# A row of lane numbers in PSUM for one-hots, and GCN rows gathered once per tile

## The reference

```python
# layer 0: relations; rel = edge type, 8 of them
row = src + n * rel
deg = segment_sum(ones, row, r * n);  msg = x[dst] * (1.0 / deg)[row][:, None]
agg = segment_sum(msg, row, r * n).reshape(r, n, e)
out0 = relu(einsum('rij,rnj->ni', weights, agg))

# layer 1: GCN
deg = 1.0 + segment_sum(ones, dst, N);  dinv = rsqrt(deg);  h = x @ W
msgs = (dinv[src] * dinv[dst])[:, None] * h[src]
agg = segment_sum(msgs, dst, N) + h / deg[:, None]
out1 = batch_norm(leaky_relu(agg + b))
```

## Time and profile before

| what | value |
|---|---|
| median of 3 runs | 4256.2 us (4242.35 to 4259.15) |
| the profiled execution, its own time | 4245.88 us |
| its span, first to last instruction | 4244.1 us |
| granted TensorE clock, mean | 0.821 of full speed |
| busy: TensorE, VectorE, GpSimd, ScalarE | 74%, 63%, 59%, 19% |
| instructions | 59998 |

### The profile page before, as it was taken

One profiled execution on the slowest core, in us unless ns is written; L12 is line 12 of the kernel. 1 busy time (PEld: TensorE's weight loads), 2 busy tenths in 40 slices (PEclk: granted clock), 3 DMA queues, 4 the chain that ended last, 5 costly groups with the idle time before them and its releaser, 6 DMA issues. The chain is left out here.

```text
span 4244.1 us, 59998 instructions
## 1 busy us (share of the span) xinstructions
PE 3122.9 (74%) x14813; PEld 1957.0 (46%) x14814; DVE 2654.0 (63%) x8500; ACT 801.6 (19%) x2009; POOL 2499.5 (59%) x2771
## 2 busy tenths in 40 slices
PE   6988976636666635999997899965676876667773
PEld 3445865424444421444443344453354663345652
DVE  8986754351111249788887888884375774365875
ACT  3840000010000003000000677650010110010111
POOL 0027777737777605766663788703777751777760
PEclk8985556768888857999998999987887987889886
DMA  1111222221111112666662222203687863677871
GB/s 63 51 49 45 56 56 56 54 47 51 51 51 51 42 31 64 173 166 166 164 169 72 62 69 67 60 7 106 182 237 193 257 199 87 182 215 216 254 227 48
DMA packets 383723, 466.66 MB, mean 110 GB/s; under 512 B 56179, under 2 KB 284944, under 8 KB 383482
## 3 DMA queue, kind: packets, MB, share of 16 engines
q0 software_dynamic: 84864, 219.09, 20.9%
q1 hardware_dynamic: 298618, 244.58, 19.0%
HBM read 349.37 MB, written 114.10 MB: 109 GB/s over the span
## 5 line engine op out<-in xcount | busy, mean ns | idle before, releaser
L1844 POOL DMA_INDIRECT got<-kv_table,pair_src x832 | 824.7, 991 | 552.9 <-issue 368.1
L603 POOL DMA_INDIRECT y_got<-y_table,y_idx x416 | 450.0, 1082 | 404.7 <-POOLq L57 278.2
L1009 POOL DMA_INDIRECT got<-t_table,pair_src x416 | 412.6, 992 | 192.8 <-issue 126.2
L2055 PE MATMUL psum<-acc 125*128 x1664 | 288.0, 327 | 204.5 <-DVE h L1907 180.2
L1203 PE MATMUL sums<-msg,hot 128*125 128x512 f32 x832 | 404.5, 635 | 29.4 <-POOL msg L1144 29.4
L2067 PE MATMUL psum<-h,acc 128*128 128x128 f32 x1664 | 331.2, 335 | 77.2 <-ACT hot_b L2031 53.1
L1431 POOL DMA_INDIRECT got<-x_table,pair_src x312 | 294.3, 943 | 154.9 <-issue 152.0
L2055 PEld LDWEIGHTS psum<-acc 125*128 125x128 f32 x1664 | 248.2, 227 | 280.6 <-issue 279.5
L1019 DVE TENSOR_TENSOR hot<-pair_dst,iota 128x500 f32<-128x500 f32 x112 | 76.0, 684 | 457.2 <-PE gcn_psum L1085 456.8
L1470 DVE SCALAR_TENSOR_TENSOR small<-z,att 128x128 f32<-128x128 f32 x1248 | 287.0, 286 | 94.0 <-PE z L1535 94.0
L1907 DVE TENSOR_TENSOR h<-psum,got 128x512 f32<-128x512 f32 x208 | 143.1, 688 | 316.6 <-DMA got<-kv_table,pair_src 284.7
(11 more groups left out here) (490 smaller groups left out, 5724.5 us busy)
## 6 DMA issues: line engine op xcount, KB each, us to landing
v_rows<-got SPq DMA_DIRECT2D x208, 256.0 KB, 3.8
small<-v_rows SPq DMA_DIRECT2D x208, 256.0 KB
dst_row<-dst_rows SPq DMA_DIRECT2D x312, 125.0 KB
rows<-x_rows SPq DMA_DIRECT2D x104, 256.0 KB, 2.6
x_rows<-got SPq DMA_DIRECT2D x104, 192.0 KB, 2.1
got<-kv_table,pair_src POOLq DMA_INDIRECT x832, 4.1
y_table<-y_stage SPq DMA_DIRECT2D x25, 500.0 KB
y_got<-y_table,y_idx POOLq DMA_INDIRECT x416, 2.6
```

Of the source, the lines that this page charges most:

```text
L603: pool.indirect_dma_start(out=got[:, slot, j, :], out_offset=None, in_=y_table[:, :], in_offset=bass.IndirectOffsetOnAxis(ap=m.y_idx[:, co ...
L1009: pool.indirect_dma_start(out=self.got[:, slot, j, :], out_offset=None, in_=self.table[:, :], in_offset=bass.IndirectOffsetOnAxis(ap=self. ...
L1844: pool.indirect_dma_start(out=got[:, slot, j, :], out_offset=None, in_=kv_table[:, :], in_offset=bass.IndirectOffsetOnAxis(ap=m.pair_src[: ...
L2055: last = t.matmul(work[:, j * P:(j + 1) * P], hot_t[:, g % 2, j // 2, j % 2, :], m.acc[:, bass.ds(ws[j], 1), 0:D].rearrange("q o d -> q (o ...
```

## The change

1. Counting compares against a copy of the row of lane numbers in a PSUM bank (`ps[2]`), the GCN one-hots against one in a bank of their own (`iota_psum`).
2. GCN rows are gathered once per tile: 392 gathers by `tile_src` (made in `sort_edges`, one more operation there) in place of 416. They go into a ring of NS = 12 groups of four tiles, and a pair's product reads the slot (p - window) mod 48, a number that VectorE works out before (`slot_i`) and TensorE loads into a register, as it does the window's. Gather group g waits until pair group g - 6 is used. TensorE waits for tile group g before pair group g, and for nothing from group 98 on.
3. The 6 matmuls of zeros stay only behind pair groups 0 to 91.
4. The GCN loops of TensorE and VectorE are written out in place of loops of 13 rounds.
5. The ring of layer 0 has 33 groups, not 34, which also starts its `keep_busy` two groups earlier.

```diff
-YS, Y_EARLY, SL, RB = 6, 6, 34, 104
+YS, Y_EARLY, SL, RB = 6, 6, 33, 104
+NS, ROOM = 12, (W - 1) // 4
...
             dve.wait_ge(lanes_done, 1)
+            go(v.tensor_scalar(m.tile_src[:, :], lanes[0][:, 0:TILES], float(N - 1), None, ALU.min))
...
+            link(v.tensor_copy(ps[2][:, 0:P], m.iota[:, 0:P]))
             for g in range(groups):
...
-                v.tensor_tensor(hot_c[:, g % 4, :, :], bc_last(src_loc[:, g * G:(g + 1) * G], P), bc_mid(m.iota[:, 0:P], G),
+                v.tensor_tensor(hot_c[:, g % 4, :, :], bc_last(src_loc[:, g * G:(g + 1) * G], P), bc_mid(ps[2][:, 0:P], G),
...
-            loop.gathers(pool, lambda g, slot: pool.wait_ge(used, g + 1))
+            for g in range(tile_groups):
+                if g >= NS:
+                    pool.wait_ge(used, g - NS + ROOM + 1)
+                for j in range(G):
+                    col = g * G + j
+                    pool.indirect_dma_start(out=got[:, col % ring, :], out_offset=None, in_=table[:, :],
+                                            in_offset=bass.IndirectOffsetOnAxis(ap=m.tile_src[:, col:col + 1], axis=0)
+                                            ).then_inc(come[g % NS], 16)
...
+            def one_hots(g):
+                v.tensor_tensor(hot[:, g % 8, :, :], bc_last(m.pair_dst[:, g * G:(g + 1) * G], Q), bc_mid(iota[:, 0:Q], G),
+                                ALU.is_equal).then_inc(hot_ready, 1)
+
+            link(v.tensor_copy(iota[:, 0:Q], m.iota[:, 0:Q]))
+            link(v.tensor_tensor(slot_f[:, :], m.iota[0:1, 0:PAIRS], m.pair_win[0:1, :], ALU.subtract))
+            link(v.tensor_scalar(turn_f[:, :], slot_f[:, :], 1.0 / ring, 0.5 / ring - 0.5, ALU.mult, ALU.add))
+            link(v.tensor_scalar(turn_f[:, :], turn_f[:, :], ROUND, None, ALU.add))
+            link(v.tensor_scalar(turn_f[:, :], turn_f[:, :], ROUND, None, ALU.subtract))
+            link(v.scalar_tensor_tensor(slot_f[:, :], turn_f[:, :], -float(ring), slot_f[:, :], ALU.mult, ALU.add))
+            v.tensor_copy(slot_i[:, :], slot_f[:, :]).then_inc(slots_ready, 1)
+            for g in range(8):
+                one_hots(g)
...
+            pe.wait_ge(slots_ready, 1)
+            for g in range(groups):
+                ws = windows(nc, m.pair_win_i, ENG.PE, g * G, G)
+                at = windows(nc, slot_i, ENG.PE, g * G, G, ring - 1)
+                pe.wait_ge(hot_ready, g + 1)
+                if g < tile_groups:
+                    pe.wait_ge(come[g % NS], 16 * G * (g // NS + 1))
+                for j in range(G):
+                    last = t.matmul(sums[0:Q, bass.ds(ws[j] * D, D)], hot[:, g % 8, j, :],
+                                    got[:, bass.ds(at[j], 1), :].rearrange("l o d -> l (o d)"), start=False, stop=False)
+                last.then_inc(used, 1)
+                if g < tile_groups - ROOM:
                     keep_busy(t, sums[0:Q, 6 * 512:7 * 512], zeros, Q, 6)
             clear_banks(t, zeros, sums, True).then_inc(done, 1)
```

More of the change, by code:

```diff
@@ L212, in common @@
     m.pair_win = sb("pair_win", [P, PAIRS])
+    m.tile_src = sb("tile_src", [P, TILES], U32)
     m.pair_win_i = sb("pair_win_i", [1, PAIRS], I32)
@@ L978, with windows @@
 WG = 2 * G
-def windows(nc, wins, engine, at, n):
+def windows(nc, wins, engine, at, n, top=W - 1):
     cols = slice(at, at + n) if isinstance(at, int) else bass.ds(at, n)
     _, values = nc.values_load_multi_w_load_instructions(
-        wins[0:1, cols], engines=[engine], min_val=0, max_val=W - 1, skip_runtime_bounds_check_because="a pair's window is a count of 24 comparisons")
+        wins[0:1, cols], engines=[engine], min_val=0, max_val=top, skip_runtime_bounds_check_because="a pair's window is a count of 24 comparisons")
     return values
@@ L1033, in gcn_sums @@
         sb, sem, bank = scope(nc, ctx)
-        loop = PairLoop(nc, m, ctx, table, hots=8)
+        ring, come, groups, tile_groups = NS * G, m.come_tile, PAIRS // G, TILES // G
+        got, hot = sb("got", [P, NS * G, D]), sb("hot", [P, 8, G, Q])
+        slot_i, slot_f, turn_f = sb("slot_i", [1, PAIRS], I32), sb("slot_f", [1, PAIRS]), sb("turn_f", [1, PAIRS])
+        hot_ready, slots_ready = sem("hot_ready"), sem("slots_ready")
         zeros = sb("zeros", [P, 512], BF16)
-        sums = m.gcn_psum
+        sums, iota = m.gcn_psum, bank("iota_psum")
         used, zeroed, done = sem("used"), sem("zeroed"), sem("all_summed")
@@ L1053, in _ @@
         def _(pool):
-            loop.gathers(pool, lambda g, slot: pool.wait_ge(used, g + 1))
+            for g in range(tile_groups):
[6 more added lines that the diff above has]
+                                            ).then_inc(come[g % NS], 16)
+            for i in range(NS):
+                pool.wait_ge(come[i], 16 * G * ((tile_groups - i + NS - 1) // NS))
         @block.vector
@@ L1058, in _ @@
             nc.vector.memset(zeros[:, :], 0.0).then_inc(zeroed, 1)
-            for slot in range(loop.slots):
-                loop.one_hots(slot * G, slot)
+            v = nc.vector
             link = make_link(dve, chain)
+            def one_hots(g):
[10 more added lines that the diff above has]
+                one_hots(g)
             dve.wait_ge(loaded, 48)
@@ L1065, in _ @@
             link(nc.vector.tensor_tensor(m.x_beta[:, :, :], m.x[:, :, :], bc_mid(m.gcn_vec[0:Q, 2, :], W), ALU.add))
[L1066 to L1070, removed]
+            for g in range(8, groups):
+                dve.wait_ge(used, g - 7)
+                one_hots(g)
             dve.wait_ge(done, 1)
@@ L2157, in build @@
         common(m, sb)
-        m.come = [[sem(f"come{n}_{b}") for b in range(8)] for n in range(4)]
+        m.come = [[sem(f"come{n}_{b}") for b in range(8)] for n in range(3)]
+        m.come_tile = [sem(f"come_tile{b}") for b in range(NS)]
         m.come_y = [sem(f"come_y{b}") for b in range(SL)]
```

## The result

The changed kernel takes 4196.2 us (median, 4194.04 to 4197.35) against 4249.3 us of the kernel before measured beside it: a ratio of 0.9874, 95% interval 0.9847 to 0.9901, 53 us less. The forecast was a ratio of 0.9886 and 4208 us in a range of 4192 to 4234. The profiled execution has a span of 4194.1 us, 50.0 us less than before, where the sum said 48.5.

A forecast was written before the change was run, and what follows sets the result against it. GpSimd's gathers, lengthened by VectorE operations with both inputs in SBUF, were taken to bound layer 0's queue and the GCN sum. Terms -20.2 and -28.3 us gave -48.5, ratio 0.9886, 4208 us; range 4192 to 4234.

The forecast's parts named there:

- The bound and the mechanism: Layer 0's queue and the GCN sum follow GpSimd; one-hots with both inputs in SBUF lengthen gathers from 0.94 to 1.40 us.
- Layer 0: Sorting and layer 0 together: -22.0 us of counting's lead, +1.2 lost again, +0.6 for sorting, so -20.2 us.
- The catch-up: Layer 0's main loop: TensorE starts waiting for rows 8 groups later, at group 57, about 600 us; costs 1.2 us.
- the extra operation: Sorting: one more VectorE operation from PSUM, 392 columns, adds 0.6 us.
- GCN gathers: GCN sum: 24 fewer gathers, -29.9 us, and less lengthening by one-hots, net -11.1 us.
- the operations for slot_i: GCN start: new VectorE operations of some 3 us, covered, that may hold up gathers by 1.0 us.
- The GCN end: Last GCN gather to TensorE's end: landing, seven groups at half clock and clearing, 19.5 us, so +12.7 us.
- The landing: GCN end: rows of the last gather reach TensorE 1.8 us after it.
- the stages behind are unchanged: Everything after the GCN sum keeps its time: 0 us.
- A: Counting and GCN: a PSUM operand doesn't free the gathers; total -15.6 us, 4241 us; chance 7%.
- C: GCN sum: TensorE becomes the bound through loads and register operations; 4304 us at 5.8 us per group; chance 4%.
- B: Layer 0: counting's lead is lost again by a full ring, TensorE at half clock or slow landings; 4228 us; 7%.

The follow-up runs named there:

- gcn_psum: Kernel before with only the GCN one-hots reading the row of lane numbers from PSUM: 4238.6 us, ratio 0.9963.
- count_psum_2: Kernel before with only counting's one-hots reading the row of lane numbers from PSUM, on a chip of normal speed: 4228.5 us, ratio 0.9943.
- wide_psum: Changed kernel with the three wide GCN operations (3200 columns) reading their small operand from PSUM copies: 4197.2 us, 3.7 us under the changed kernel's repeat.
- both_more: Changed kernel with one-tensor-input degree one-hots and the wide GCN operations' small operand in PSUM: 4167.6 us, ratio 0.9801 to the kernel before.
- second and third set: Follow-up runs on two chips of normal speed; the kernel before took 4254.2 and 4253.7 us there.
- tiles_only_2: Changed kernel with both comparisons reading SBUF again, on a chip of normal speed: 4235.0 us, ratio 0.9961 to the kernel before.
- first set: Follow-up runs on a chip where VectorE and TensorE stood still again and again; the kernel before took 5065.9 us there.
- deg_scalar: Changed kernel with layer 0's degree one-hots built by eight operations with one tensor input instead of two with two: 4174.6 us, ratio 0.9811 to the kernel before.
- count_psum: Kernel before with only counting's one-hots reading the row of lane numbers from PSUM, on the slow chip: 5062.7 us, ratio 0.9999.

## Why the prediction was right, point by point

**The bound and the mechanism** were as told: both stages follow GpSimd, VectorE operations with both inputs in SBUF hold up gathers, those with one in PSUM don't. Rows 4 had shown it; `gcn_psum`, `count_psum_2` and `wide_psum` confirm it one at a time.

**The parts.** Against the kernel before, single parts gave 25.2 (counting), 15.7 (GCN one-hots) and 18.7 us (tiles and end), together 59.6 against 53 for all at once; each has an interval of about 6 us to either side, so the two agree. The sum had 20.8, 11.1 and 29.9 - 12.7 = 17.2. Within the last part only the zeros were tried by themselves; writing the loops out and the ring of 33 were not.

**Layer 0.** Forecast -20.2 up to the GCN stage. Its first gather moved from 924.50 to 902.36, -22.1. The catch-up came at 610 us instead of 600: group 59 for 57. GpSimd's start was late by 1.4 us (283.1 against 281.7), where 0.6 was added for the extra operation. No run shows that term by itself: with the operation in, the starts of other runs lie between 281.6 (`both_more`) and 285.4 us (`wide_psum`), without it at 282.1 and 282.2.

**GCN gathers.** From the first one's start to the last one's end 539.1 us before, 497.0 after: -42.1, forecast -41.0. Of that, the operations for slot_i cost 0.3 us (two gathers of 1.11) where 1.0 was taken.

**The GCN end** is the term that was mis-sized. Forecast 19.5 us from the last gather to the end of TensorE, with the seven groups at half clock throughout. Measured from 1399.34: 2.8 us to the first product (taken 1.8), 9.4 for the seven groups (14.4) and 1.7 for the clearing (3.25): 13.9 us, 5.6 less. Two things were wrong in the 14.4. Without a pause, groups at half clock start less than 2.06 us apart: the first four of the block start at 1402.15, 1404.01, 1405.72 and 1407.43. And the clock didn't stay at half: these products came without a pause, and it rose in the fourth group, so the next starts are 1408.73, 1409.60 and 1410.60. From these starts, an estimate: seven groups at the pace of the first three (5.28 us) would have taken 12.3 us, so some 2 of the 5.0 us are the first thing and some 3 the clock. The six groups lay near the low bound (7 us). The landing was misread by 1.0 us the other way, and the rows of before had it: for the last gather of all it was already 1466.40 - 1463.58 = 2.8 us, and the 1.8 is that of group 101. The two loads of window and slot per group didn't show.

**The rest was not unchanged in the profiled execution.** From the first operation behind the GCN sum to the end the trace before has 2771.1 us and the one after 2779.2. The other profiled executions of the second and third set lie between 2772.9 (`gcn_psum`) and 2782.2 us (`tiles_only_2`). They overlap, but not without order: the three kernels with the old GCN loops have 2771.1 to 2776.2 us, the seven profiles with the new ones 2773.4 to 2782.2, on the mean 5 us more. So part of the 8 us may be a cost of the change that the sum put at nothing ("the stages behind are unchanged"); one profile of each run can't tell that from scatter. Some 6 of the 8 us arise in the two transformer convolutions, which no kernel touched, and their cause stays open. The surplus of the GCN end and of layer 0 was offset by this, and the closeness of 48.5 and 50.0 is in part luck.

**The rivals.** A fell. C too: TensorE waited 187.1 us for rows in the GCN stage. B didn't happen on the chips where the kernel takes 4250 us. On the chip of the first set, where the main loop began late, the ring did fill, and counting's row in PSUM alone gained nothing.

## What to carry to other kernels

An engine that only issues gathers can be the bound of a stage while the page shows it 59% busy (76% within the GCN stage, where most of the rest is the gap of 0.30 us behind each gather): compare the duration of one gather where it is alone with that beside each kind of VectorE operation, and change what lengthens it, even hundreds of us ahead of where the gain shows. Moving the small, constant operand of a comparison into a spare PSUM bank cost VectorE nothing (0.69 us before and after) and gave 0.4 to 0.6% a place here. A lead is worth something only while the ring behind it isn't full, so check the ring's level at the consumer's start.

## What the runs showed of the hardware that was not expected

A run of 56 products without pause began at half clock and ended at full clock, with no zeros to help, and took 9.58 us; with 6 zeros behind each group the third group was the first wholly at full clock, and the seven took 18.2 us.

A gather can be held through more than one operation: 8.8 us in `tiles_only_2`, where the longest VectorE operation beside it is 3.5 us. Eight short bf16 operations with one tensor input lengthen gathers too, but far less than the two they replaced: the gathers that overlap them lose 6.2 us in all in `deg_scalar` (163 gathers), those that overlap the two operations 29.4 us in the changed kernel (118).

On one chip VectorE and TensorE stood still 13.3 us at a time in counting, and the same kernel took 5066 us instead of 4250. A change of 0.6% elsewhere measured as 0.0% there. What the engines lacked isn't shown: it happened in written-out code and in loops alike (in `count_psum` VectorE stood 340 us in the GCN loop of 13 rounds, again "remote"), and the queues that bring instructions moved the same as in the profile of the kernel before (124 packets and 2.03 MB on one, 117 and 0.96 MB on the other).
